# Graph network on one core: the third softmax partly prepared in the scores stage and run in two pieces, GpSimd weighting 3 of 8 items of the third sums, edgeless rows seeded in the sum banks, the last stage spread over four engines

## The reference

```python
def gat_conv(h, src, dst, fc_w, attn_l, attn_r, bias, heads, out_feats):
    feat = (h @ fc_w.T).reshape(n, heads, out_feats)
    e = leaky_relu(el[src] + er[dst], 0.2)
    ex = exp(e - segment_max(e, dst)[dst])
    a = ex / segment_sum(ex, dst)[dst]
    return segment_sum(feat[src] * a[..., None], dst) + bias
...
# layer 3 (relational attention over the edges, 4 heads of 64)
scores = einsum('ehd,ehd->eh', Q[dst], K[src] + 0.2 * rel[:, None, :]) / D ** 0.5
ex = exp(scores - segment_max(scores, dst)[dst])
w = ex / segment_sum(ex, dst)[dst]
agg = segment_sum(w[:, :, None] * V[src], dst)
msgs = where(deg[:, None, None] > 0, agg, V)
out = msgs.reshape(N, H * D) @ Wo + bo
x = layernorm(out + node_features) * gamma + beta
return layernorm(node_features + x)
```

## Time and profile before

| | |
|---|---|
| runs | 2234.57 us median (2231.8 to 2241.07) |
| profiled execution | 2232.32 us, span 2230.6 us |
| PE | 1509.1 us busy (68%) |
| PE weight loads | 1137.5 us (51%) |
| DVE | 1516.2 us (68%) |
| GpSimd (POOL) | 1273.5 us (57%) |
| ACT | 404.5 us (18%) |
| mean granted TensorE clock | 0.795 |
| DMA | 406.10 MB, mean 182 GB/s |

### The profile page before, as it was taken

How to read it: one execution, slowest core, us unless ns; L and a number is a source line. 1 busy time by engine, 2 the same in 40 slices (tenths; PEclk the granted TensorE clock), 3 DMA queues, 4 the chain that set the end, 5 groups by cost and what they waited for, 6 DMA issues and landing times. The chain is left out here.

```text
span 2230.6 us, 29002 instructions
## 1 busy us (share of the span) xinstructions
PE 1509.1 (68%) x7673; PEld 1137.5 (51%) x7674; DVE 1516.2 (68%) x2333; ACT 404.5 (18%) x735; POOL 1273.5 (57%) x1321
## 2 busy tenths in 40 slices
PE   6247567566566444886666599778777875599965
PEld 4235455455445443775455446555555554477743
DVE  3357877777775886773434376676767667698968
ACT  1100000000014001000000053443434442100124
POOL 0477777777702887577777706777777773000023
PEclk9657778778787555998877899877778777799989
DMA  3644444444405564344444428999999998577412
GB/s 99 161 133 128 127 120 128 123 123 125 111 11 170 173 173 135 106 129 118 119 119 118 123 104 270 342 345 335 344 343 339 339 339 286 196 273 272 168 43 74
DMA packets 234905, 406.10 MB, mean 182 GB/s; under 512 B 33199, under 2 KB 171621, under 8 KB 228197
## 3 DMA queue, kind: packets, MB, share of 16 engines
q0 software_dynamic: 73216, 219.89, 31.6%
q1 hardware_dynamic: 161637, 185.66, 26.3%
HBM read 330.93 MB, written 74.48 MB: 182 GB/s over the span
## 5 line engine op out<-in xcount | busy, mean ns | idle before, releaser
L840 POOL DMA_INDIRECT row_space<-tab_feat,src_i x760 | 742.8, 977 | 312.2 <-issue 230.9
L1088 PE MATMUL ps<-arena 128*128 128x257 f32 (+1 forms) x1664 | 429.5, 419 | 148.2 <-DVE arena L1933 148.2
L840 POOL DMA_INDIRECT row_space<-tab_kv,src_i x416 | 393.3, 945 | 192.6 <-issue 123.1
L1088 PEld LDWEIGHTS ps<-arena 128*128 128x128 f32 x1664 | 340.6, 210 | 230.7 <-issue 171.8
L1187 PE MATMUL ps<-arena 128*128 128x265 f32 x832 | 262.1, 482 | 115.3 <-DVE ps L2172 56.5
L1927 DVE TENSOR_TENSOR arena<-row_space,ps 128x2048 f32<-128x2048 f32 x95 | 216.6, 2280 | 161.6 <-DMA row_space<-tab_feat,src_i 161.6
L1022 PE MATMUL ps<-acc,arena 128*128 x832 | 285.6, 502 | 0.0
L1187 PEld LDWEIGHTS ps<-arena 128*128 128x128 f32 x832 | 197.1, 243 | 168.4 <-issue 123.1
L1420 ACT COPY acc<-ps 128x265 f32<-128x265 f32 (+2 forms) x75 | 28.2, 376 | 1149.3 <-PE ps L1088 580.4
L1806 DVE TENSOR_TENSOR arena<-row_space,ps 128x1024 f32<-128x1024 f32 x104 | 126.8, 1219 | 139.8 <-PE ps L1022 78.0
L1022 PEld LDWEIGHTS ps<-acc,arena 128*128 128x128 f32 x832 | 195.5, 246 | 38.0
(11 more groups left out here) (337 smaller groups left out, 2132.2 us busy)
## 6 DMA issues: line engine op xcount, KB each, us to landing
item_v<-row_space SPq DMA_DIRECT2D x52, 1024.0 KB, 8.2
row_space<-item_v SPq DMA_DIRECT2D x52, 1024.0 KB, 4.9
arena<-rows_block_dst SPq DMA_DIRECT2D x104, 128.0 KB
row_space<-tab_feat,src_i POOLq DMA_INDIRECT x760, 2.8
scores<-rows_block_dst SPq DMA_DIRECT2D x52, 128.0 KB
arena<-rows_src_low SPq DMA_DIRECT2D x52, 128.0 KB
row_space<-tab_kv,src_i POOLq DMA_INDIRECT x416
arena<-rows_type SPq DMA_DIRECT2D x52, 128.0 KB
```

The costliest lines, as they stand in the source:

```text
L840: nc.gpsimd.indirect_dma_start(rows_of_slot(s)[:, g, :], None, table, bass.IndirectOffsetOnAxis(ap=src_i[:, item:item + 1], axis=0),).then ...
L1088: last = nc.tensor.matmul(ps[:, SUM_BANKS:2 * SUM_BANKS][:, bass.ds(bs[g], 1), 0:width].rearrange("p a d -> p (a d)"), onehot[:, s % 2, g, ...
```

## The change

- `gathers(1)`: six early groups, then the eight slots of the ring, then the three spare groups; DVE takes them in the same order.
- score3: SP loads bo, gamma, beta, the key rows and nine blocks of own values (V rows of the nodes) at its beginning; DVE makes the edgeless mask `inv_deg`, the parts of bo - beta and the gap row `gap3` there.
- `soft3`: the first scan reads the transposed scores in PSUM; maxima, exponential and transposes back run in two pieces (8 and 5 chunks); ACT moves the shares straight to their banks; the first two groups' one-hots are made in this stage.
- sum3: from the third group on GpSimd weights items 0 to 2 of each group and DVE items 3 to 7; DVE copies GpSimd's shares to `scores` once (`keep_shares`). PE waits for both. A bank starts from V times the edgeless mask, with the mask itself in the denominators' columns (`seed`), not from zero. GpSimd adds beta to `base`, a block every second group.
- final: GpSimd's scaled rows go to PE directly; DVE no longer inserts V and no longer applies the inner factor and beta; ACT applies the inner factor (`scale_inner`). The first 20 blocks' denominators are inverted before the last sums have been copied. DVE's iterations are written out, with lags 0, 1, 3 and 4 in place of 2, 3, 4 and 5.

```diff
+POOLED = 3
+FIRST_SUMS = 20
+WHOLE = 2
+PIECES = ((0, 8), (8, 13))
...
@@ sync, score_rows(2, "score3")
+                    sp.dma_start(bias_row[:], a["bo"]).then_inc(weights_in[3], 16)
+                    for k, name in enumerate(["gamma", "beta"]):
+                        sp.dma_start(bias_all[:, k, :], a[name].broadcast_to([P, D])).then_inc(weights_in[3], 16)
+                    row = rows_d["dst"].rearrange("(c j) e -> c (j e)", c=P // H3)
+                    for h in range(H3):
+                        sp.dma_start(keys3[h * (P // H3):(h + 1) * (P // H3), :], row).then_inc(seg_in, 16)
+                    for b in range(EARLY_OWN):
+                        load_own(b)
...
@@ sync, soft3
+            for s in range(SLOTS):
+                load_values(0, s)
+            sp.dma_start(w_b[:], halves(a["wo"])).then_inc(weights_in[3], 16)
+            sp.wait_ge(bias_made, 1)
...
+            for b in range(EARLY_OWN, BLOCKS):
+                load_own(b)
+            for s in range(SLOTS, PREFETCH):
+                load_values(0, s)
...
@@ gpsimd, gathers
-                for k in range(first):
-                    gather_early(k)
-                for i in range(mine):
-                    gather(i // ring, i % ring)
+                if n == 1:
+                    for k in range(AHEAD):
+                        gather_early(k, k)
+                for i in range(ring):
+                    gather(i // ring, i % ring, (AHEAD if n == 1 else 0) + i)
+                if n == 1:
+                    for k in range(AHEAD, EARLY):
+                        gather_early(k, ring + k)
+                for i in range(ring, mine):
+                    gather(i // ring, i % ring, first + i)
...
+            for i in range(WHOLE, GROUPS):
+                s, z = i % PREFETCH, i % 2
+                pool.wait_ge(values_in[s], i // PREFETCH * 16 + 16)
+                pool.wait_ge(sum_mm, i * GROUP // QUAD + (2 * QUADS + TICKS + CREDIT - GROUP // QUAD))
+                nc.gpsimd.tensor_tensor(
+                    weighted[:, z, 0:POOLED, 0:D].rearrange("p i (h d) -> p i h d", h=H3),
+                    row_slots[s][:, 0:POOLED].rearrange("p i (h d) -> p i h d", h=H3),
+                    by_item(H3)[:, i * GROUP:i * GROUP + POOLED, :].unsqueeze(3).broadcast_to([P, POOLED, H3, R]),
+                    ALU.mult).then_inc(pool_weighted, 1)
+                pool.wait_ge(pool_weighted, i + 1)
+                pool.sem_inc(slot_used[s], 1)
+                if i % 2:
+                    b = i // 2 - 1
+                    nc.gpsimd.tensor_tensor(base[:, b], base[:, b], bias_all[:, 1, :], ALU.add).then_inc(pool_step, 1)
...
@@ tensor, sums
+                        if n == 2:
+                            pe.wait_ge(pool_weighted, u * SLOTS + (s + 1))
...
@@ scalar
+            def seed(b):
...
+                bank, edgeless = SUM_BANKS + b % SUM_BANKS, inv_deg[:, b:b + 1]
+                nc.scalar.activation(ps[:, bank, 0:D], own_values[b], ACT.Copy, scale=edgeless)
+                return nc.scalar.activation(ps[:, bank, D:AW], ones[:, 0:AW - D], ACT.Copy, scale=edgeless)
...
+                for piece, (lo, hi) in enumerate(PIECES):
+                    act.wait_ge(seg_dve, 3 + 3 + piece)
+                    nc.scalar.activation(top3[:, lo * P:hi * P], top3[:, lo * P:hi * P], ACT.Exp).then_inc(seg_exp, 1)
+                act.wait_ge(seg_back, 2)
+                move(0, 4)
+                did(move(4, 8))
+                for b in range(2):
+                    seed(b).then_inc(bank_free, 1)
+                act.wait_ge(seg_back, 3)
+                did(move(8, 12))
+                move(12, 13).then_inc(seg_copied, 1)
...
-            pipeline(nc.scalar.Fori, [(0, copy_transposes(2)), (2, deviation(1, 0)), (5, normalise), (4, deviation(0, 1))])
+            pipeline(nc.scalar.Fori, [(0, copy_transposes(2)), (1, deviation(1, 0)), (2, scale_inner), (4, deviation(0, 1)), (5, normalise)])
...
@@ vector, sums
+                    made = vec.tensor_tensor(weighted[:, z, pooled:, 0:D].rearrange("p i (h d) -> p i h d", h=heads),
+                                             taken[:, pooled:].rearrange("p i (h d) -> p i h d", h=heads),
+                                             share[:, pooled:].unsqueeze(3).broadcast_to(
+                                                 [P, GROUP - pooled, heads, D // heads]), ALU.mult)
```

369 lines of the change are left out of this document (225 added, 144 removed).

## The result

The changed kernel takes 2170.82 us in the median of four runs (2170.51 to 2171.3), against 2235.4 for the kernel before beside it (four runs, 2231.8 to 2241.07): a ratio of 0.9709, 95% interval 0.9688 to 0.973, so 64.6 us less. Forecast were 2177 us and a range of 2163 to 2196.

What follows compares the result with a forecast made beforehand. It took GpSimd's gathers to pace the second sums and layer 3's scores, and DVE's build the third sums, PE close behind. Terms -12.1 + 3 - 7.9 - 8.0 - 12.2 - 17.0 - 1 = -55.2 gave 2177 us, range 2163 to 2196.

Steps and rivals of the forecast that it cites:

- Gather order: Second sums: GpSimd's one pause in its gathers goes whole, -12.1 us, bounds -12.4 and 0.
- Preparation in layer 3's scores: Start of layer 3's scores: later query copies on DVE make a slot late for GpSimd, +3 us, bounds 0 and +8.
- Third softmax: From layer 3's scores to the first sums product: earlier scan and two pieces start PE sooner, -7.9 us, bounds -10 and -4.
- Third sums: Third sums: DVE's shorter build makes PE the bound, 24 pairs from 185.1 to 177.1 us, -8.0, bounds -10 and 0.
- Head: Last bank's copy to first statistics: inverses no longer wait, bias parts and weights are loaded; -12.2 us, bounds -13 and -8.
- Steady part: Last stage's 24 blocks: a two-block cycle of 4.7 us, 2.4 a block taken, -17.0 us, bounds -24 and -3.
- Tail: From the last statistics to the end: one operation less on DVE, -1 us, bounds -2 and +1.
- A: Last stage: stays near 3.0 us a block, engine hops and GpSimd's hold closing the loop; +14, 2191 us; chance 0.15.
- B: Third sums: gain nothing, PE's bank loads or second wait taking the 0.4 us; +8, 2185 us; chance 0.10.
- D: Second sums: GpSimd's pause only moves behind group 16; +12, 2189 us; chance 0.06.
- C: Layer 3's start: GpSimd stalls 20 us rather than 3, own values crowding out first item rows; 2194 us; chance 0.06.
- E: Third sums and last stage: DVE and GpSimd exclude each other on every instruction; 2254 us; chance 0.03.

Runs made afterwards that it cites:

- old_order: The changed kernel with only layer 2's gather order put back (nine early groups, then the ring): 2184.5 us.
- dve_extra: The changed kernel with one more 256-element addition on DVE, its result unused, ahead of each block's outer factor in the last stage: 2181.1 us.
- pool1: The changed kernel with GpSimd weighting one item of a group instead of three, DVE seven, in the third sums: 2179.8 us.
- pool5: The changed kernel with GpSimd weighting five items of a group instead of three, DVE three, in the third sums: 2168.8 us.

## Why the prediction was right

The sign and the range held, and five of the seven terms lay within their bounds; the forecast gain was 7 us too small, mainly by the third sums and the steady part.

- *Gather order*, -12.1: measured -12.0 at the first gather of layer 3. The mechanism is shown by old_order; that it agrees to 0.1 us is luck. The pause kept 1.55 us of its 12.41, the 136 gathers ahead of it took 3.1 us less, and the node stage behind took 2.4 more, and both of these lie within what they scatter over kernels with the same code (206.6 to 210.9 us, 67.1 to 71.3). In the other kernels with the new order the pause was 2.8 us or less, and none in nine.
- *Preparation in layer 3's scores*, +3: 3.3 us of stall, +4.0 over the gathers, within 0 to +8. The step named the slack as 10.8 us and the shift as 8 to 13, "since PE waits in between and may restart at half clock". DVE's copies came 12 us later, PE did restart at half clock, and this decided between 0.7 and 3.3 us. The further 1.7 us behind the last gather lie within what this tail scatters over runs.
- *Third softmax*, -7.9: -7.7, through the steps named: the first scan starts 2.35 us earlier (2.4). What the step did not have is the 0.8 us for which PE waits for GpSimd's signal.
- *Third sums*, -8.0: -12.2. The step "PE becomes the bound. What remains is its gap at a pair's start" was right. Mis-sized was PE's own time, by a reading of the earlier trace rows: 7.28 us there is a pair from its first start to the end of its last record. That record lasts 0.38 us, but the next can start 0.22 after it, as they do all through the pair. So PE's own pair was 7.12 us in the kernel before already, and DVE's build cost it 0.57 a pair and not 0.4. With the gap of 0.42 us once in two pairs a pair now takes 7.28 instead of the 7.38 taken, 2.4 us over 24. Most of the rest is in the first two pairs, which the step left at their old length: by the starts of the records 17.7 us before and 16.4 now.
- *Head*, -12.2: -11.9. Of this 10.3 us are waiting, 7.4 of them for the inverses and the parts, and 1.6 are PE at full clock instead of half, which the step had as "at the clock of the sums". Fetching and inserting V, the likely rest of the waiting, was not tried alone.
- *Steady part*, -17.0: -21.1. The cycle was named and measured: 4.57 us for two blocks where 4.7 was worked out. Wrong was the allowance for "GpSimd's hold on the outer factor", which raised 2.35 to 2.4: the factor now runs just ahead of the add and takes 0.13 us. And the first four blocks go at PE's pace, 1.88, before the cycle fills, which the step left out: 2.28 a block behind them, 2.23 in the mean.
- *Tail*, -1: -2.7, just outside its bound. DVE's work counts in it, since dve_extra lengthens it by 2.4 us; more was not looked into.

Of the rivals, A (3.0 a block), B (no gain in the sums) and D (the pause moves) did not come. C named the right place, but the stall did not come near 20 us; with the same own values it is 0.7 us at full clock. E, that DVE and GpSimd exclude each other on every instruction, falls with the line of DVE's times in pool1, changed and pool5; for an operation with its inputs in SBUF dve_extra shows the hold. Not settled is what costs PE 0.42 us at a turn of the sums.
